# Row units of the attention scores: forty ahead of the attention steps instead of thirty-two, the other 216 spread evenly

## The chip, the cores and the metric

One NeuronCore of a Trainium2 chip runs the whole kernel. The metric is the device time of one execution in microseconds; the median of three runs of the kernel before is 518.95 us (518.05 to 519.51). Its engines work in parallel, each through its own queue in order: TensorE (PE in the profile) does matmuls into PSUM, VectorE (DVE) and ScalarE (ACT) read PSUM and compute elementwise, GpSimd (POOL) helps, and the DMA queues move data. They wait for each other on semaphores.

## The reference

One transformer layer on x, 1024 tokens by 512 features. With `xn = layernorm(x)` the result is `x + attention(xn) + ffn(xn)`:

```
q, k, v = bitnet_linear(xn, ...)     # sign(weight) matmul, times mean|weight| * scale
                                     # 32 query heads, 8 key/value heads, head size 16
attn    = softmax(q @ k.T / sqrt(16))
out     = bitnet_linear(attn @ v, o_weight, o_scale)
ffn     = (silu(xn @ gate.T) * (xn @ up.T)) @ down.T      # 1792 hidden features
```

The softmax of each query row subtracts that row's maximum over the 1024 keys, so the maxima have to be known before the exponentials are taken.

## The kernel before, in words

**Two stages.** The front does the layernorm, the projections of q, k and v, and the gate and up matmuls of the feed-forward part. The attention steps follow, then the output projection and the down projection.

**Row units.** Heads are taken in 8 groups of 4 query heads that share a key head; a group is two half-blocks of 512 queries, so there are 16 blocks. Before a block's scores can be shifted by their row maxima, the maxima are computed by 16 *row units*, 256 in all. A unit `A n` is 128 queries of one head against all 1024 keys: two matmuls of 512 keys (line 1081, `half_rows`, one in the upper and one in the lower half of the array's rows) into one of two pairs of PSUM banks (unit number modulo 2), then one VectorE reduction of 128x1024 (line 796, `row_max`). The semaphore `rows_ready` releases the reduction; `rows_free` releases the matmuls of unit n once the reduction of unit n-2 is done, since it uses the same bank pair. When all 16 maxima of a block are there, `transpose_max` (line 1092) turns them, ScalarE copies them (line 582), and two GpSimd operations split them.

**Attention steps.** There are 128 steps, 8 per block. A step (`scores`, `exps`) has four score matmuls (line 1165), each 128 keys by 512 queries into one of three banks, four exponentials on ScalarE (line 663), and the products of the probabilities of the step before with the values (`times_values`, line 1200; 16 records a step, in two halves). Score and row matmuls alternate between the halves of the array's rows. At the end of each block ScalarE copies the products out (line 674). In the 112 steps of the first seven groups the kernel also computes, two units a step, the row units of the next group: the first unit's matmuls stand beside scores 0 and 1, the second's beside scores 2 and 3. The last 16 steps have no row units; parts of the down projection fill them.

**The order of the front.** It is written out by hand, one string for TensorE (`pe_order`), one for VectorE (`dve_order`) and one for ScalarE. `F w` is a gate and an up half (16 matmuls of 512 columns, line 1072; on VectorE line 891, on ScalarE lines 644 and 576). `S 1` sums the magnitudes of the output weights with an fp32 matmul (line 1012) into bank 0 and makes the output scale on VectorE (lines 862, 864 and 867); `SUM_AT` is the first unit behind it, whose matmuls wait for `factors_ready`, which line 864 gives, because they write bank 0 again. `T 0` is the transposition of block 0's maxima, into bank 6. The feed-forward unit w waits for the VectorE result of unit w-2 (`h_ready`), and the one behind `T 0` also for ScalarE's copy of the maxima (`max_taken`). The first attention step's scores wait for `h_ready` too, its third one for all 28.

Of the kernel before, what the change touches and what calls it, by code (L numbers as in the profile page):

```python
# [27 lines left out]
def layer_kernel(nc, x, wq, wk, wv, wo, sq, sk, sv, so, gate, up, down, sg, su, sd, out,  # L28
# [18 lines left out]
    NG = NKV  # L47
    NP = NG // 2
    STEPS = 2 * TT
    FU = 2 * FT  # L50

    assert KV == P and HC * P == H and QT * P == NH * D and TT % 4 == 0
# [6 lines left out]
    pe_order = ("K0 X0 X1 X2 X3 K1 S0 X4 X5 G0 X6 Z0 X7 U0 P0 Z1 P1 Z2 G1 P2 U1 F2 F3 P3 F4 P4 F5 P5 F6 F7 A0 F8 F9 "  # L59
                "A1 A2 F10 F11 A3 A4 F12 A5 A6 F13 A7 S1 F14 A8 A9 F15 A10 A11 F16 A12 A13 F17 A14 A15 F18 A16 F19 "  # L60
                "A17 A18 F20 T0 A19 A20 F21 A21 A22 F22 A23 F23 A24 A25 F24 A26 A27 F25 A28 A29 F26 A30 A31 F27 ")
    dve_order = ("M0 M1 J0 M2 M3 H0 M4 R0 N0 J1 N1 M5 N2 N3 M6 M7 H1 L0 R1 L1 N4 N5 L2 L3 S0 Z0 N6 N7 J2 L4 V0 L5 L6 "
                 "Z1 L7 F0 Z2 g0 G0 Z3 X0 g1 F1 G1 E2 F2 X1 F3 g2 G2 g3 G3 F4 g4 F5 X3 G4 F6 F7 A0 g5 F8 G5 F9 X4 "
                 "F10 A1 A2 A3 F11 A4 X5 A5 A6 F12 A7 S1 F13 A8 F14 A9 F15 A10 A11 F16 A12 A13 A14 F17 A15 A16 F18 "
                 "F19 A17 A18 A19 A20 F20 F21 A21 F22 A22 A23 F23 A24 A25 F24 A26 A27 A28 A29 F25 F26 A30 A31 F27 ")
    act_order = ("D0 B0 C0 B1 B2 D1 C1 C2 N2 C3 C4 C5 W0 C6 N0 C7 F0 N1 E0 E1 X0 F1 F2 X1 Y0 F3 E3 F4 V2 E4 F5 X3 F6 "
# [16 lines left out]
    for order in (pe_order, dve_order):  # L83
        assert [n for kind, n in order if kind == "A"] == list(range(2 * UNITS))
    assert [n for kind, n in act_order if kind == "F"] == list(range(FU))
# [36 lines left out]
    def exps_before(e):  # L122

        return e - 2 if e - 3 < T_ENTRY else max(e - 3, T_ENTRY)

    def at(gp, s):
# [5 lines left out]
    with ExitStack() as ctx:  # L132
# [573 lines left out]
        def _(dve):  # L706
# [86 lines left out]

            def row_max(n, hf, idx):
                dve.wait_ge(rows_ready, n + 1)
                nc.vector.tensor_reduce(nmx[:, hf, idx:idx + 1], bank_pair(idx % 2), AX.X, ALU.max,  # L796
                                        negate=True).then_inc(rows_free, 1)

            splits = 0
            for kind, n in dve_order:  # L800
# [84 lines left out]
                elif kind == "F":  # L885
                    f, hf = n // 2, n % 2
                    dve.wait_ge(gt_ready, n + 1)
                    dve.wait_ge(up_ready, n + 1)
                    if n >= 2:
                        dve.wait_ge(hlo_ready, n - 1)  # L890
                    nc.vector.scalar_tensor_tensor(out=hb[:, n % 2, :], in0=ps[:, 5 + 2 * (n % 2), :],  # L891
                                                   scalar=usc[:, f:f + 1], in1=gt[:, n % 2, :],
                                                   op0=ALU.mult, op1=ALU.mult).then_inc(h_ready, 1)
                elif kind == "V":


                    dve.wait_ge(factors_ready, 2)
                    step(nc.vector.tensor_reduce(vg[:, 0:1], svb[:, :], AX.X, ALU.max, apply_absolute_value=True))
                    step(nc.vector.tensor_scalar(vg[:, 1:2], vg[:, 0:1], float(H), TOP, ALU.mult, ALU.min))
                    step(nc.vector.tensor_scalar(vg[:, 2:3], vg[:, 1:2], TINY, 1.0 / VTOP, ALU.max, ALU.mult))  # L900
                    nc.vector.reciprocal(vg[:, 3:4], vg[:, 2:3]).then_inc(vscale_ready, 1)
                elif kind == "A":
                    row_max(n, n // UNITS, n % UNITS)

            def step_rows(gp, s, last):

                gp_, par, hf, j = at(gp, s)
                with_rows = not (last and (par == 1 or s == 2 * STEPS))
                ga_ = gp_ * 2 + par + 1
                if with_rows:  # L910
                    row_max(ga_ * (2 * UNITS) + hf * UNITS + 2 * j, hf, 2 * j)
                    row_max(ga_ * (2 * UNITS) + hf * UNITS + 2 * j + 1, hf, 2 * j + 1)

# [35 lines left out]

            step_rows(0, 0, False)  # L950
            for gp in range(NP - 1):
                for s in range(1, 2 * STEPS + 1):
                    step_rows(gp, s, False)
            for s in range(1, 2 * STEPS):
                step_rows(NP - 1, s, True)
                if s in O_INVERT:
                    invert(O_INVERT.index(s))
                if s in O_NORM:
                    normalize_output(O_NORM.index(s))
                if s in O_SPLIT:  # L960
                    o_low(O_SPLIT.index(s))
                if s in D_OUT:
                    down_out(D_OUT.index(s))
# [12 lines left out]
        def _(pe):  # L976
# [99 lines left out]

            def half_rows(par, hf, idx, b):

                head, qt = idx // (HALF // P), idx % (HALF // P)
                low = b * HI  # L1080
# [3 lines left out]

            def rows(n, par, hf, idx):
                pe.wait_ge(rows_free, n + 1)
                half_rows(par, hf, idx, 0)
                half_rows(par, hf, idx, 1).then_inc(rows_ready, 1)

# [4 lines left out]
            for kind, n in pe_order:  # L1094
# [15 lines left out]
                elif kind == "A":  # L1110
                    if n == 0:
                        pe.wait_ge(y_ready, len(PROJ))
                        pe.wait_ge(kA_loaded[0], 32)
                    if n % UNITS == 0:
                        pe.wait_ge(q_loaded[0][n // UNITS], 32)
                    if n == SUM_AT:
                        pe.wait_ge(factors_ready, 3)
                    rows(n, 0, n // UNITS, n % UNITS)
                elif kind == "T":
# [18 lines left out]
            def scores(gp, s, last, opening=False):  # L1138
# [8 lines left out]
                with_rows = not (last and par == 1)  # L1147
                if with_rows and j == 0:
                    pe.wait_ge(q_loaded[1 - par][hf], 32 * (gp_ + par + 1))
                    if hf == 0:  # L1150
                        pe.wait_ge(kA_loaded[1 - par], 32 * (gp_ + par + 1))
                if not with_rows:
                    fill = list(range(len(FILLS) * (s - STEPS) // STEPS, len(FILLS) * (s - STEPS + 1) // STEPS))
                transposes = not (last and s >= STEPS + TT)
                for i, r in enumerate(ROUND):
# [7 lines left out]
                    if opening and i == 2:  # L1163
# [3 lines left out]
                                     qst[low:low + SROWS, par, hf, r, :], start=True, stop=True).then_inc(scores_ready, 1)  # L1167
                    idx = 2 * j + i // 2
                    if with_rows and i < REP - 1:
                        if i % 2 == 0:  # L1170
                            pe.wait_ge(rows_free, (gp_ * 2 + par + 1) * (2 * UNITS) + hf * UNITS + idx + 1)
                        mm = half_rows(1 - par, hf, idx, 1 - half)
                        if i % 2 == 1:
                            mm.then_inc(rows_ready, 1)
                        if i == REP - 2:
                            half_rows(1 - par, hf, idx, half).then_inc(rows_ready, 1)
                    if i % 2 == 1 and with_rows and not opening:
# [110 lines left out]
```

## Time and profile before

| | |
|---|---|
| median of 3 runs | 518.95 us |
| profiled execution | 519.96 us, of which 518.2 us lie between its first and last instruction (the span) |
| TensorE busy | 493.8 us (95%) |
| VectorE busy | 418.3 us (81%), of it 293.3 us in the 256 reductions |
| ScalarE busy | 351.1 us (68%), of it 274.2 us in the 512 exponentials |
| chain that ended last | 83% TensorE, 7% ScalarE, 4% VectorE |

The span is from the first to the last instruction; 1.76 us of the profiled execution lie around it. Records overlap: a matmul of 512 columns is shown with some 380 ns, while the next one starts 216 ns behind it, so distances between starts tell the pace, not the mean durations. The same holds for a reduction, shown with 1.21 us. In this execution the front reaches to 160.59 us, where the first score matmul starts; the last step with row units ends near 420 us.

### The profile page before, as it was taken

How to read it: one execution, taken by the hardware profiler on the slowest of the kernel's cores; microseconds unless marked ns; L12 is line 12 of the kernel's file. 1: busy time of each engine (PE TensorE's matmuls, PEld its weight loads, DVE VectorE, ACT ScalarE, POOL GpSimd, SP SyncE). 2: the span in 40 equal slices, each digit the busy share in tenths (PEclk: the TensorE clock that was granted, in tenths of full speed). 3: DMA queues.
4: the chain of work that ended last, by engine and by line, in shares of the span. 5: the costliest groups of instructions: out<-in, count | busy, mean ns of one | idle time of the engine just before them, and what ended most of it. 6: DMA issues, size and time to landing. Idle time of an engine off the chain costs nothing.

```text
span 518.2 us, 9807 instructions
## 1 busy us (share of the span) xinstructions
PE 493.8 (95%) x3928; PEld 170.9 (33%) x3928; DVE 418.3 (81%) x483; ACT 351.1 (68%) x639; POOL 97.4 (19%) x140
## 2 busy tenths in 40 slices
PE   2899999999999999999999999999999999999995
PEld 1866444433432222222222222222222222223442
DVE  7459866876678999999999999999999942224795
ACT  2373545222337999999999999999999986774000
POOL 4200424744424000000000000000000121241031
PEclk9999999999999999999999999999999999999999
DMA  8901482443100911202102120110210214451321
GB/s 278 214 2 59 119 198 44 102 79 43 22 1 7 165 34 42 60 23 61 40 25 59 40 60 23 53 47 24 61 40 23 66 44 114 95 170 48 98 82 40
DMA packets 29956, 36.37 MB, mean 70 GB/s; under 512 B 6544, under 2 KB 20752, under 8 KB 29912
## 3 DMA queue, kind: packets, MB, share of 16 engines
q1 hardware_dynamic: 20888, 24.72, 16.0%
q0 software_dynamic: 8304, 10.95, 11.1%
q8 instruction: 31, 0.51, 0.4%
q10 hardware_dynamic: 720, 0.08, 0.1%
q14 instruction: 13, 0.11, 0.1%
HBM read 30.62 MB, written 10.35 MB: 79 GB/s over the span
## 4 chain that ended last, share of the span: by engine, by line
PE 83%; ACT 7%; DVE 4%; DMA 3%; issue 2%; SPq 1%; ACTq 0%; DVEq 0%
PE ps L1200 23%; PE ps L1072 19%; PE ps L1165 14%; PE ps L1133 9%; PE ps L1081 8%; ACT room L663 5%; PE ps L1051 3%; PE ps L1226 3%; DVE nmx L796 3%; PE ps L1004 2%; DMA room<-wq 2%; ACT osb L674 1%; DMA ga<-r_scratch 1%; PE ps L1043 1%; SPq L384 1%
## 5 line engine op out<-in xcount | busy, mean ns | idle before, releaser
L796 DVE TENSOR_REDUCE nmx<-ps 128x1 f32<-128x1024 f32 x256 | 293.3, 1213 | 9.9 <-PE ps L1081 9.7
L663 ACT ACTIVATE room<-ps 128x512 f32<-128x512 f32 x512 | 274.2, 597 | 21.3 <-PE ps L1165 11.2
L1200 PE MATMUL ps<-room,vcur 128*32 128x256 f32 (+1 forms) x1912 | 160.0, 406 | 4.4 <-ACT osb L674 4.2
L1165 PE MATMUL ps<-qst,kB 50*128 50x512 f16 x512 | 150.2, 383 | 2.5 <-ACT room L663 1.8
L1081 PE MATMUL ps<-kA,qst 48*128 48x512 f16 x512 | 145.3, 382 | 0.0
L1072 PE MATMUL ps<-room,wf 128*128 128x512 f16 x448 | 101.5, 381 | 0.0
L1200 PEld LDWEIGHTS ps<-room,vcur 128*32 128x32 f32 x1912 | 37.7, 108 | 99.9 <-issue 52.7
L1165 PEld LDWEIGHTS ps<-qst,kB 50*128 50x128 f16 x512 | 30.9, 93 | 114.5 <-ACT room L663 101.5
L644 ACT ACTIVATE room<-ps,gsc 128x512 f32<-128x512 f32 x28 | 19.2, 686 | 63.6 <-PE ps L1072 63.6
L1072 PEld LDWEIGHTS ps<-room,wf 128*128 128x128 f16 x448 | 42.5, 98 | 55.4 <-issue 8.0
L502 POOL TENSOR_TENSOR hlo<-room,hhi 128x512 f16<-128x512 f32 x28 | 34.1, 1216 | 98.2 <-ACT hhi L576 98.2
L508 POOL TENSOR_TENSOR shp<-mxs,ones 16x128 f16<-16x128 f32 x16 | 7.2, 448 | 226.9 <-ACT mxs L582 226.9
L1133 PE MATMUL ps<-wd,hhi 128*128 128x512 f16 x112 | 42.6, 380 | 0.0
L1133 PE MATMUL ps<-wd,hlo 128*128 128x512 f16 x112 | 42.5, 380 | 0.0
L891 DVE SCALAR_TENSOR_TENSOR room<-ps,usc,room 128x512 f32<-128x512 f32 x28 | 20.9, 747 | 21.5 <-PE ps L1072 10.7
L924 DVE TENSOR_TENSOR y<-y,ga 128x1024 f32<-128x1024 f32 (+1 forms) x5 | 5.1, 1012 | 33.4 <-DMA ga<-r_scratch 33.4
L1081 PEld LDWEIGHTS ps<-kA,qst 48*128 48x128 f16 x512 | 27.2, 94 | 7.5 <-issue 6.7
L576 ACT CAST hhi<-room 128x512 f16<-128x512 f32 x28 | 17.1, 610 | 2.1 <-DVE room L891 2.1
L1051 PE MATMUL ps<-room,sgn 128*128 128x512 f16 x80 | 18.0, 379 | 0.0
L1133 PEld LDWEIGHTS ps<-wd,hhi 128*128 128x128 f16 x112 | 10.9, 98 | 13.2 <-issue 1.8
L1133 PEld LDWEIGHTS ps<-wd,hlo 128*128 128x128 f16 x112 | 10.9, 98 | 13.1 <-issue 1.8
L461 POOL TENSOR_TENSOR room<-room,parts 128x512 f32<-128x512 f32 x6 | 8.5, 1421 | 35.3 <-DVE room L936 29.6
(128 smaller groups left out, 289.2 us busy)
## 6 DMA issues: line engine op xcount, KB each, us to landing
qst<-q_scratch SPq DMA_DIRECT2D x32, 192.0 KB, 3.4
o_scratch<-osb SPq DMA_DIRECT2D x16, 256.0 KB, 2.3
q_scratch<-parts SPq DMA_DIRECT2D x12, 256.0 KB
hlo<-x SPq DMA_DIRECT2D x8, 256.0 KB, 4.7
parts<-x POOLq DMA_DIRECT2D x8, 256.0 KB, 2.9
wf<-gate POOLq DMA_DIRECT2D x14, 128.0 KB, 3.7
wf<-up POOLq DMA_DIRECT2D x14, 128.0 KB, 4.0
wd<-down POOLq DMA_DIRECT2D x1, 1792.0 KB, 13.7
```

What stands on the lines that cost most here:

```text
L502: nc.gpsimd.tensor_tensor(hlo[:, f, hf * HALF:(hf + 1) * HALF], hb[:, w % 2, :], hhi[:, f, hf * HALF:(hf + 1) * HALF], ALU.subtract).then_ ...
L576: nc.scalar.copy(hhi[:, f, hf * HALF:(hf + 1) * HALF], hb[:, n % 2, :]).then_inc(hhi_ready, 1)
L644: nc.scalar.activation(gt[:, n % 2, :], ps[:, 4 + 2 * (n % 2), :], ACT.Silu, scale=gsc[:, f:f + 1]).then_inc(gt_ready, 1)
L663: nc.scalar.activation(probs[:, s % 2, r, :], ps[:, score_bank(entry(j, i)), :], ACT.Exp, scale=gam_reg[par][r]).then_inc(scores_free, 1)
L796: nc.vector.tensor_reduce(nmx[:, hf, idx:idx + 1], bank_pair(idx % 2), AX.X, ALU.max, negate=True).then_inc(rows_free, 1)
L891: nc.vector.scalar_tensor_tensor(out=hb[:, n % 2, :], in0=ps[:, 5 + 2 * (n % 2), :], scalar=usc[:, f:f + 1], in1=gt[:, n % 2, :], op0=ALU. ...
L1051: mm = nc.tensor.matmul(ps[:, 2 * (n % 2) + hf, :], sgn[:, c, c0:c0 + P], xs[:, c, hf * HALF:(hf + 1) * HALF], start=(c == 0 and xs is xhi ...
L1072: mm = nc.tensor.matmul(ps[:, 4 + 2 * (w % 2) + z, :], wf[:, f % WF_BUFS, z, c * P:(c + 1) * P], xs[:, c, hf * HALF:(hf + 1) * HALF], star ...
L1081: return nc.tensor.matmul(ps[:, 2 * (idx % 2) + b, :], qst[low:low + KROWS, par, hf, head, qt * P:(qt + 1) * P], kA[low:low + KROWS, par, ...
L1133: mm = nc.tensor.matmul(ps[:, i, :], (hhi, hlo)[part][:, f, i * P:(i + 1) * P], wd[:, f, :], start=(f == 0 and part == 0), stop=(f == FT - ...
L1165: nc.tensor.matmul(ps[:, score_bank(e), :], kB[low:low + SROWS, par, kt % (TT // 2) * P:(kt % (TT // 2) + 1) * P], qst[low:low + SROWS, pa ...
L1200: mm = nc.tensor.matmul(ps[32 * r:32 * r + 32, 7, of], vcur[:, par, key_tile(r, j), :], probs[:, s % 2, r, of], start=(j == 0 and part == ...
```

## The change

The number of row units in the front goes from 32 to 40 (`AHEAD = 8`), so the front also computes half of block 2's. The remaining 216 units are dealt to the 112 steps by a formula: step t gets the units from 40 + 216 t / 112 up to 40 + 216 (t+1) / 112, rounded down. That is two units in 104 steps and one unit in eight: steps 0, 14, 28, 42, 56, 70, 84 and 98. Block, half and buffers of a unit now follow from its number (`row_block`), and the waits for the loaded queries and keys go with the unit that needs them first (`rows_loaded`). In the strings of the front, the units from A8 on are placed in pairs, two between every two F, and their neighbours change at three places, shown below. The core of the diff:

```diff
+    AHEAD = 8
...
-    pe_order: "... A5 A6 F13 A7 S1 F14 A8 A9 F15 ... A17 A18 F20 T0 A19 A20 F21 ... A30 A31 F27"
+    pe_order: "... A5 A6 F13 A7 S1 A8 A9 F14 A10 A11 F15 ... F20 A22 A23 T0 A24 A25 F21 ... A36 A37 F27 A38 A39"
...
+    ROW_STEPS = (NG - 1) * STEPS
+    OPEN_ROWS, ALL_ROWS = 2 * UNITS + AHEAD, NG * 2 * UNITS
+
+    def row_units(t):
+
+        first, end = [OPEN_ROWS + (ALL_ROWS - OPEN_ROWS) * (t + e) // ROW_STEPS for e in range(2)]
+        return list(range(first, end)) if t < ROW_STEPS else []
...
-            step_rows(0, 0, False)
+            step_rows(0, 0)
...
+            def rows_loaded(n):
+
+                gp, par, hf, idx = row_block(n)
+                if idx == 0:
+                    pe.wait_ge(q_loaded[par][hf], 32 * (gp + 1))
+                    if hf == 0:
+                        pe.wait_ge(kA_loaded[par], 32 * (gp + 1))
...
+                units = row_units(gp * (2 * STEPS) + s)
+                for n in units:
+                    rows_loaded(n)
...
-                    idx = 2 * j + i // 2
-                    if with_rows and i < REP - 1:
+                    if i < REP - 1 and i // 2 < len(units):
+                        n = units[i // 2]
                         if i % 2 == 0:
-                            pe.wait_ge(rows_free, (gp_ * 2 + par + 1) * (2 * UNITS) + hf * UNITS + idx + 1)
-                        mm = half_rows(1 - par, hf, idx, 1 - half)
-                        if i % 2 == 1:
+                            pe.wait_ge(rows_free, n + 1)
+                        mm = half_rows(n, 1 - half)
+                        if i == REP - 2:
+                            mm = half_rows(n, half)
+                        if i > 0:
                             mm.then_inc(rows_ready, 1)
-                        if i == REP - 2:
-                            half_rows(1 - par, hf, idx, half).then_inc(rows_ready, 1)
```

(The two lines of `pe_order` are cut to the places that change their neighbours. VectorE's string follows: behind `A7 S1` it now has A8 and A9 ahead of F13, at the transposition `F19 A22 A23 F20 A24 A25 F21`, and at the end `F26 A36 A37 F27 A38 A39`.)

TensorE at S 1, before. Line 1012 is S 1, lines 1072 are a feed-forward unit, lines 1081 the row units A7 (above) and A8, A9 (below).

```order
L1081 MATMUL ps<-kA,qst 128x512
L1012 MATMUL ps<-room,ones 128x512 [waits rows_free,mag_ready]
L1072 MATMUL ps<-room,wf 128x512 [waits h_ready,xlo_ready,wf_loaded3]
L1072 MATMUL ps<-room,wf 128x512 x15
L1081 MATMUL ps<-kA,qst 128x512 [waits rows_free,factors_ready]
L1081 MATMUL ps<-kA,qst 128x512
L1081 MATMUL ps<-kA,qst 128x512 [waits rows_free]
```

The same place in the changed kernel, where S 1 is line 1025, a feed-forward unit 1085 and a row unit 1095.

```order
L1095 MATMUL ps<-kA,qst 128x512
L1025 MATMUL ps<-room,ones 128x512 [waits rows_free,mag_ready]
L1095 MATMUL ps<-kA,qst 128x512 [waits rows_free,factors_ready]
L1095 MATMUL ps<-kA,qst 128x512
L1095 MATMUL ps<-kA,qst 128x512 [waits rows_free]
L1095 MATMUL ps<-kA,qst 128x512
L1085 MATMUL ps<-room,wf 128x512 [waits h_ready,xlo_ready,wf_loaded3]
```

The sixteen matmuls of F14 stood between S 1 and the wait for `factors_ready`; now they stand behind it.

TensorE at the transposition (line 1092), before: F20, T 0, then A19 and A20, then F21.

```order
L1072 MATMUL ps<-room,wf 128x512 x15
L1092 MATMUL ps<-ident,nmx 16x128 [waits rows_free,h_ready]
L1081 MATMUL ps<-kA,qst 128x512 [waits rows_free]
L1081 MATMUL ps<-kA,qst 128x512
L1081 MATMUL ps<-kA,qst 128x512 [waits rows_free]
L1081 MATMUL ps<-kA,qst 128x512
L1072 MATMUL ps<-room,wf 128x512 [waits h_ready,max_taken,xlo_ready,wf_loaded2]
```

The same place after (line 1114 is T 0): F20, A22, A23, T 0, A24, A25, F21.

```order
L1085 MATMUL ps<-room,wf 128x512 x15
L1095 MATMUL ps<-kA,qst 128x512 [waits rows_free]
L1095 MATMUL ps<-kA,qst 128x512
L1095 MATMUL ps<-kA,qst 128x512 [waits rows_free]
L1095 MATMUL ps<-kA,qst 128x512
L1114 MATMUL ps<-ident,nmx 16x128 [waits rows_free,h_ready]
L1095 MATMUL ps<-kA,qst 128x512 [waits rows_free]
L1095 MATMUL ps<-kA,qst 128x512
L1095 MATMUL ps<-kA,qst 128x512 [waits rows_free]
L1095 MATMUL ps<-kA,qst 128x512
L1085 MATMUL ps<-room,wf 128x512 [waits h_ready,max_taken,xlo_ready,wf_loaded2]
```

Two more units stand between F20 and F21, so four share two bank pairs with no feed-forward unit between them.

TensorE where the steps open, before: F27, then step 0 (line 1165 scores, each but the last with row matmuls behind it).

```order
L1072 MATMUL ps<-room,wf 128x512 x15
L1165 MATMUL ps<-qst,kB 128x512 [waits kB_loaded0,q_loaded10,shift_loaded00,kA_loaded1,q_loaded00,scores_free,kones_ready,h_ready]
L1081 MATMUL ps<-kA,qst 128x512 [waits rows_free]
L1165 MATMUL ps<-qst,kB 128x512 [waits scores_free]
L1081 MATMUL ps<-kA,qst 128x512
L1165 MATMUL ps<-qst,kB 128x512 [waits h_ready,scores_free]
L1081 MATMUL ps<-kA,qst 128x512 [waits rows_free]
L1081 MATMUL ps<-kA,qst 128x512
```

After: F27, A38 and A39, then step 0 (line 1184 scores) with the single unit A40.

```order
L1085 MATMUL ps<-room,wf 128x512 x15
L1095 MATMUL ps<-kA,qst 128x512 [waits rows_free]
L1095 MATMUL ps<-kA,qst 128x512
L1095 MATMUL ps<-kA,qst 128x512 [waits rows_free]
L1095 MATMUL ps<-kA,qst 128x512
L1184 MATMUL ps<-qst,kB 128x512 [waits shift_loaded00,kB_loaded0,q_loaded00,scores_free,kones_ready,h_ready]
L1095 MATMUL ps<-kA,qst 128x512 [waits rows_free]
L1184 MATMUL ps<-qst,kB 128x512 [waits scores_free]
L1095 MATMUL ps<-kA,qst 128x512
L1184 MATMUL ps<-qst,kB 128x512 [waits h_ready,scores_free]
L1184 MATMUL ps<-qst,kB 128x512 [waits scores_free] x2
```

In front of step 0's second score stands the wait of A40 for the reduction of A38, which was issued just ahead; scores 2 and 3 have no row matmuls beside them.

## Rows read from the trace of the kernel before

**Rows 1.** Busy time of each engine by stretch: front, opening, steps.

```profile
core 0: us, PE busy (x) PEld busy (x) DVE busy (x) ACT busy (x) POOL busy (x), PEclk, DMA share, GB/s
82.00:160.00 78.00, 78.00 (x375) 31.17 (x374) 58.34 (x63) 26.49 (x43) 34.92 (x37) 1.00 0.24 45
...
182.00:402.40 220.40, 216.53 (x2320) 54.90 (x2316) 218.52 (x193) 211.87 (x409) 12.41 (x30) 1.00 0.15 42
```

**Rows 2.** Order of time, TensorE, within a block: start, us, instruction, [idle before].

```profile
247.93 0.64 PE L1200 MATMUL ps<-room,vcur 128*32 128x256 f32 x8
248.50 0.39 PE L1165 MATMUL ps<-qst,kB 50*128 50x512 f16 x1
248.51 0.60 PE L1081 MATMUL ps<-kA,qst 48*128 48x512 f16 x2
248.74 0.38 PE L1165 MATMUL ps<-qst,kB 50*128 50x512 f16 x1
249.04 0.64 PE L1200 MATMUL ps<-room,vcur 128*32 128x256 f32 x8
```

**Rows 3.** Order of time, VectorE, one block of 16 reductions.

```profile
221.94 18.21 DVE L796 TENSOR_REDUCE nmx<-ps 128x1 f32<-128x1024 f32 x16 [0.16 <-PE ps L1081]
```

**Rows 4.** Order of time, ScalarE, in the same steps and at block ends.

```profile
247.82 1.09 ACT L663 ACTIVATE room<-ps 128x512 f32<-128x512 f32 x2
...
248.99 0.60 ACT L663 ACTIVATE room<-ps 128x512 f32<-128x512 f32 x1
...
255.44 0.59 ACT L674 COPY osb<-ps 128x512 f32<-128x512 f32 x1
...
273.82 0.59 ACT L674 COPY osb<-ps 128x512 f32<-128x512 f32 x1
```

**Rows 5.** Order of time, TensorE at S 1 and behind it.

```profile
103.14 1.13 PE L1012 MATMUL ps<-room,ones 128*128 128x512 f32 x2
104.10 3.62 PE L1072 MATMUL ps<-room,wf 128*128 128x512 f16 x16
107.65 0.61 PE L1081 MATMUL ps<-kA,qst 48*128 48x512 f16 x4
108.18 3.63 PE L1072 MATMUL ps<-room,wf 128*128 128x512 f16 x16
```

**Rows 6.** Order of time, VectorE at S 1.

```profile
104.39 0.68 DVE L862 TENSOR_SCALAR ga<-ps 128x512 f32<-128x512 f32 x1
105.10 0.75 DVE L864 SCALAR_TENSOR_TENSOR sob<-sob,vg,ga 128x512 f32<-128x512 f32 x1
```

**Rows 7.** Order of time, TensorE and VectorE at T 0, and a front pair's reductions.

```profile
131.92 0.27 PE L1092 MATMUL ps<-ident,nmx 128*16 128x128 f32 x1
132.12 0.61 PE L1081 MATMUL ps<-kA,qst 48*128 48x512 f16 x4
132.66 3.63 PE L1072 MATMUL ps<-room,wf 128*128 128x512 f16 x16
...
132.56 2.35 DVE L796 TENSOR_REDUCE nmx<-ps 128x1 f32<-128x1024 f32 x2 [1.47 <-PE ps L1081]
```

**Rows 8.** Order of time, TensorE, VectorE and ScalarE where the steps open.

```profile
160.59 0.39 PE L1165 MATMUL ps<-qst,kB 50*128 50x512 f16 x1
...
161.65 0.37 PE L1165 MATMUL ps<-qst,kB 50*128 50x512 f16 x1 [0.45 <-DVE room L891]
...
163.98 0.64 PE L1200 MATMUL ps<-room,vcur 128*32 128x256 f32 x8 [0.19 <-ACT room L663]
...
160.75 0.75 DVE L891 SCALAR_TENSOR_TENSOR room<-ps,usc,room 128x512 f32<-128x512 f32 x1 [1.08 <-issue]
...
161.80 2.04 ACT L663 ACTIVATE room<-ps 128x512 f32<-128x512 f32 x4
```

**Rows 9.** Waits of TensorE and busy time by stretch near the start.

```profile
PE ps L983 <- DVE room L744: 4.0, 1, 4.0
...
0.00:40.00 40.00, 28.53 (x135) 21.97 (x136) 24.32 (x70) 17.14 (x22) 8.96 (x21) 1.00 0.57 160
```

## What the change will do: the prediction

> **What bounds the kernel now.** I read four views: busy time by stretch, to see which engines are full; the order of time within a block, for the true pace of each; the order of time at the three places where neighbours change; and the waits. By stretch [rows 1], TensorE is full in the front (78.00 of 78.00 us), while VectorE is not (58.34). Whatever is put on TensorE's queue there, work or waiting, comes out at the end one for one. In the steps three engines look full: TensorE 216.5, VectorE 218.5 and ScalarE 211.9 of 220.4 us. Busy shares can't say which of them sets the pace, so the distances between starts must.
>
> A half step on TensorE goes from products to products, 247.93 to 249.04: 1.11 us, with no idle time shown [rows 2]. In it two scores and two row matmuls take 0.54 us (248.50 to 249.04), which is two matmuls one behind the other and not four: each score shares its time with a row matmul in the other half of the array's rows (starts 0.01 apart). The sixteen reductions of a block take 18.21 us [rows 3], so they follow each other at (18.21 - 1.21) / 15 = 1.133 us. They are slower than TensorE's 1.11 and fall behind inside a block by 16 x 0.023 = 0.4 us; the two bank pairs take this up, and at the block's end TensorE waits for ScalarE's copy and VectorE catches up (0.16 us idle [rows 3]). A block lasts 273.82 - 255.44 = 18.38 us [rows 4]: 16 x 1.11 = 17.76 and 0.6 for copy and transposition. If reductions set the pace, the half steps would be 1.13 apart, and they are 1.11. So I take TensorE as the bound, VectorE just behind it (18.13 + 0.16 of 18.38) and ScalarE also near.
>
> **The change part by part.** Three terms lengthen the front, one lengthens the opening of the steps, one shortens the steps.
>
> *First, work in the front.* Behind S 1 and ahead of F27 stand 30 units instead of 24. A pair of units takes 108.18 - 107.65 = 0.53 us on TensorE [rows 5]. Three more pairs are 1.6; they stand at one place more between feed-forward units, 0.1 for the change between the two kinds of matmul (an estimate; below 0.2 in any case, since a whole pair costs 0.53). Together 1.7 us. VectorE hides their reductions: a pair takes 2.35 [rows 7] and its feed-forward product 0.7, in a period of 3.55 + 0.53 = 4.08 us.
>
> *Second, the wait at S 1.* A8 waits for `factors_ready`, since it writes the bank that S 1 filled. Line 864 gives it at 105.10 + 0.75 = 105.85 [rows 6]. F14 started at 104.10, right behind S 1, and covered this completely [rows 5]. Now A8 stands there, and everything behind it in TensorE's queue with it: 105.9 - 104.1 = 1.8 us lost. Nothing else could run, for the queue is in order.
>
> *Third, the wait at T 0.* Without F between them, A22 to A25 share two bank pairs. Counted from A22's first matmul, the reductions begin after 132.56 - 132.12 = 0.44 and take 2.35 for two [rows 7]: done at 1.65 and 2.79. A25 needs the second, so it starts at 2.8 and F21 some 0.3 behind it, at 3.1. Unhindered the two pairs and T 0 would take 0.54 + 0.20 + 0.54 = 1.28 [rows 7]. Loss 1.8 us. `max_taken` is long there by then.
>
> So F27 ends 1.7 + 1.8 + 1.8 = 5.3 us later than in the profile before.
>
> *Fourth, the opening.* Before, the first score starts right at F27's end (160.59), and ScalarE takes exponentials from 161.80 on without a break, four in 2.04 us [rows 8]. Counting from F27's end, the product of F27 is at 0.16 on VectorE [rows 8]; behind it the reduction of A38 starts at 0.8 and ends at 2.05. A40 waits for it, and score 1 stands behind A40: it starts at 2.1 and is ready at 2.5, where ScalarE could have taken it at 1.2 + 0.5 = 1.7. The next ones follow 0.5 apart, so the exponentials of step 0 come 0.8 us late, and step 1's products with them. Step 0 has one unit only, so VectorE, which has A38 to A42 to do from 0.8 on, is through with A41 at 0.8 + 4 x 1.13 = 5.3, before step 2 asks for it (near 6): no further loss. I take 0.8 (0.3 if ScalarE catches up with its spacing of 0.48 against 0.55 in the steps, 1.5 if A41 and A42 hold TensorE too).
>
> *Fifth, the eight steps with one unit.* Step 0 is counted. In the other seven, scores 2 and 3 stand alone, in different halves, and can run side by side: at most 0.22 us of TensorE's 0.54 goes. But the products wait for the last exponential of the step before: two exponentials end at 247.82 + 1.09 = 248.91 [rows 4], and the products begin at 249.04 [rows 2]. Of 0.13 some 0.1 is to be had. 7 x 0.09 = 0.6 us; bounds 0 (it is lost at the next copy) and 7 x 0.22 = 1.5. The eight reductions that leave, 8 x 1.13 = 9 us of VectorE, buy nothing more, since it isn't the bound.
>
> The waits for queries and keys that now come up to four steps (9 us) earlier cost nothing: queries are reloaded when their block's scores are done, and the new units need them half a block (9.2 us) later.
>
> The sum is 5.3 + 0.8 - 0.6 = 5.5 us. Against the profiled execution, 519.96, of which 1.76 lie around the span, it gives 525.5; the median of the runs is 1.0 us below that execution, so I predict 518.95 + 5.5 = 524.4 us. With the ends of each term (front 4.3 to 6, opening 0.3 to 1.5, steps -1.5 to 0) the case reaches from 522.3 to 526.3.
>
> **The rivals.**
>
> *Reductions set the steps' pace (faster).* For it: VectorE is busy 99% of the steps [rows 1], with 0.16 us idle a block [rows 3]. If TensorE's half step is only as short as the bank pairs allow, the 216 units take 8 x 1.13 = 9.0 us less than the 224, and 524.4 + 0.6 - 9.0 = 516.0 comes out. It decides from the point where more than 6 of the 9 us are given back, at any of the seven steps. Against it: the half steps lie 1.11 apart, which is less than a reduction. Chance 0.06. The Trainium skill, "TensorEngine Tiling (Array Packing)", section Performance Considerations, says the same as this rival in general: tiling makes TensorE faster but not the emptying of PSUM, so the read of PSUM may become the bottleneck. By that rule 516 would come; rows 2 and 3 put TensorE first by 0.02 us a half step.
>
> *One of the two waits doesn't arise.* If the units around T 0 or at S 1 find what they need in time, 1.8 us go: 522.6, and without both 520.8. For S 1 line 864 would have to be faster than shown; for T 0 the reductions. Neither has a reason in the rows. Chance 0.08.
>
> *TensorE's clock falls in the waits.* If it were granted the lower of its levels, 1.2 instead of 2.4 GHz, behind each wait, the sixteen matmuls that follow (3.55 us [rows 5]) would take 3.5 us longer each: 524.4 + 7 = 531. Against it: a wait of 4.0 us near the start left the granted clock at 1.00 [rows 9]. Chance 0.03. [...]
>
> The forecast itself has 0.83.
>
> **How the numbers follow.** A run of this kernel can be told from no change at about 0.3%, 1.6 us: 517.4 to 520.5. Faster: the rival with the reductions, 0.06. Same: part of the case without both waits and of a half-true reduction rival, 0.03. Slower: the rest, 0.91. The range goes from 521.3, so that it takes in the case with one wait missing, to 526.3; what is left out is the reductions, part of the second rival and the clock, and some 0.05 of larger terms than I see.
>
> **What would show it.** In the profile after: TensorE waits of 1.8 us for VectorE line 881 behind line 1025, and of 0.9 and 0.8 us for reductions (line 813) in front of A24 and A25, between F20 and F21; the first score (line 1184) near 166.5; the second one 1.5 us behind it; blocks of 18.37 us without a one-unit step and 0.1 less with one; VectorE idle about 1.1 us at each such step. I am wrong if blocks become shorter than 18.2 throughout (reductions were the bound), or if the front ends before 164 (the waits are not there).

## The result, and the profile after

The changed kernel is slower: 528.73 us median of six runs (527.21 to 531.89) against 519.88 us of the kernel before in the same comparison. The ratio is 1.0164, with its 95% interval [1.0136, 1.0193], so 8.5 us, where 5.5 was forecast, and the time lies above the range (521.3 to 526.3). The profiled execution took 531.89 us, of it 530.1 span. It is the longest of the six.

The busy line and the clock line of the page of after (40 slices of 13.25 us; a 9 stands for 90% or more):

```profile
PE 500.8 (94%) x3928; PEld 172.4 (33%) x3928; DVE 420.0 (79%) x483; ACT 351.8 (66%) x639; POOL 97.5 (18%) x140
...
PEclk9999999999899799999999999999999998999999
```

Three slices are below 9, where the kernel before had none: at about 138, 173 and 442 us. The busy time by stretch, of the first two and of what lies between them, and then of the steps (columns as in [rows 1], the granted clock third from the end):

```profile
138.50:141.80 3.30, 3.30 (x9) 1.18 (x8) 1.71 (x2) 1.19 (x2) 0.00 (x0) 0.50 0.06 9
141.90:172.50 30.60, 28.56 (x147) 10.73 (x145) 22.88 (x23) 11.40 (x20) 9.33 (x11) 1.00 0.01 1
172.60:179.30 6.70, 6.70 (x41) 1.25 (x41) 4.14 (x4) 4.12 (x9) 3.25 (x5) 0.50 0.53 77
...
193.00:413.00 220.00, 215.64 (x2302) 55.28 (x2302) 212.30 (x186) 211.66 (x409) 12.43 (x30) 1.00 0.15 41
```

A granted clock of 0.50 is the lower level, 1.2 GHz. In the steps the clock is full again and VectorE has fallen from 99% to 96.5% busy.

Who waited, TensorE in after (us in total, times, longest):

```profile
PE ps L1219 <- ACT osb L690: 4.4, 13, 0.5
...
PE ps L1095 <- DVE nmx L813: 2.9, 3, 1.3
PE ps L1184 <- ACT room L679: 2.1, 2, 1.6
PE ps L1095 <- DVE sob L881: 1.7, 1, 1.7
```

The kernel before has no waits for the reductions (there line 796) or for the S 1 product (line 864). They are the waits of the forecast, at its three places. In order of time, TensorE at S 1 and at T 0 (compare [rows 5, 7]):

```profile
103.05 1.12 PE L1025 MATMUL ps<-room,ones 128*128 128x512 f32 x2
105.83 0.60 PE L1095 MATMUL ps<-kA,qst 48*128 48x512 f16 x4 [1.65 <-DVE sob L881]
106.37 3.63 PE L1085 MATMUL ps<-room,wf 128*128 128x512 f16 x16
...
134.51 0.60 PE L1095 MATMUL ps<-kA,qst 48*128 48x512 f16 x4
135.04 0.28 PE L1114 MATMUL ps<-ident,nmx 128*16 128x128 f32 x1
136.22 0.39 PE L1095 MATMUL ps<-kA,qst 48*128 48x512 f16 x2 [0.90 <-DVE nmx L813]
137.35 0.39 PE L1095 MATMUL ps<-kA,qst 48*128 48x512 f16 x2 [0.74 <-DVE nmx L813]
137.67 5.31 PE L1085 MATMUL ps<-room,wf 128*128 128x512 f16 x16
142.92 0.61 PE L1095 MATMUL ps<-kA,qst 48*128 48x512 f16 x4
```

A8 starts 2.78 us behind S 1 instead of 0.96. F21 starts 3.16 us behind A22, where 3.1 was worked out. But then F21 takes 142.92 - 137.67 = 5.25 us where every other one takes 3.56: half the clock for 3.4 us costs 1.7.

Where the steps open (compare [rows 8]), and the first steps:

```profile
167.94 0.38 PE L1184 MATMUL ps<-qst,kB 50*128 50x512 f16 x1
169.60 0.39 PE L1095 MATMUL ps<-kA,qst 48*128 48x512 f16 x2 [1.28 <-DVE nmx L813]
169.83 0.59 PE L1184 MATMUL ps<-qst,kB 50*128 50x512 f16 x3
...
173.50 1.08 PE L1219 MATMUL ps<-room,vcur 128*32 128x256 f32 x8
...
179.60 0.64 PE L1219 MATMUL ps<-room,vcur 128*32 128x256 f32 x8
```

Score 1 comes 1.9 us behind score 0, where 1.5 was forecast. At 173.50 the products take 1.08 us and at 179.60 again 0.64: half the clock in between.

The steps themselves. A half step with two scores and no row unit, and the next ones:

```profile
236.85 0.64 PE L1219 MATMUL ps<-room,vcur 128*32 128x256 f32 x8
237.42 0.42 PE L1184 MATMUL ps<-qst,kB 50*128 50x512 f16 x2
237.77 0.64 PE L1219 MATMUL ps<-room,vcur 128*32 128x256 f32 x8
238.34 0.39 PE L1184 MATMUL ps<-qst,kB 50*128 50x512 f16 x1
...
238.98 0.64 PE L1219 MATMUL ps<-room,vcur 128*32 128x256 f32 x8
...
240.09 0.64 PE L1219 MATMUL ps<-room,vcur 128*32 128x256 f32 x8
```

The first half step is 0.92 us instead of 1.11, the next one 1.21 and then 1.11 again: 0.19 won, 0.10 given back at the next step's products. VectorE in a block without a one-unit step and behind one, and ScalarE's copies at the ends of another block (compare [rows 3, 4]):

```profile
214.18 18.22 DVE L813 TENSOR_REDUCE nmx<-ps 128x1 f32<-128x1024 f32 x16 [0.15 <-PE ps L1095]
...
239.02 11.66 DVE L813 TENSOR_REDUCE nmx<-ps 128x1 f32<-128x1024 f32 x10 [0.72 <-PE ps L1095]
```

```profile
265.97 0.59 ACT L690 COPY osb<-ps 128x512 f32<-128x512 f32 x1
...
284.26 0.59 ACT L690 COPY osb<-ps 128x512 f32<-128x512 f32 x1
```

284.26 - 265.97 = 18.29 us is a block with a one-unit step (42) in it, 0.09 less than the 18.38 of before; blocks without one stay at 18.37. VectorE idles 0.72 us at a one-unit step (1.1 was forecast), and the block is not shorter by that.

Comparing every step's first exponential in the two traces, counted from S 1's first matmul, gives where the time of the three profiles is, 9.1 to 12.0 us at their ends:

| place (us) | profile of after | second and third profile | forecast |
|---|---|---|---|
| F27's last matmul | +7.0 | +7.0, +7.0 | +5.3 |
| of it, F21 at half clock | 1.7 | 1.7, 1.7 | |
| opening, step 0 to 1 | +1.1 | +1.1, +1.1 | +0.8 |
| opening, steps 1 to 3 | +2.7 | +1.2, +1.2 | 0 |
| one-unit steps | -0.54 | -0.55, -0.51 | -0.6 |
| steps 112 to 118 | +2.0 | +0.5, -0.1 | 0 |

### The profile page after: what moved, and what is told of

Read it like the earlier page. It is cut to its first block, busy times and chain, and to the rows that moved or that the text cites. A ratio compares the mean times of both kernels' runs of the same rounds, so it can differ in the third digit from the quotient of the medians.

```text
span 530.1 us, 9807 instructions
## 1 busy us (share of the span) xinstructions
PE 500.8 (94%) x3928; PEld 172.4 (33%) x3928; DVE 420.0 (79%) x483; ACT 351.8 (66%) x639; POOL 97.5 (18%) x140
## 4 chain that ended last, share of the span: by engine, by line
PE 77%; ACT 10%; issue 5%; DMA 3%; DVE 2%; POOL 1%; SPq 1%; ACTq 0%; POOLq 0%; DVEq 0%
PE ps L1219 21%; PE ps L1085 19%; PE ps L1184 12%; ACT room L679 9%; PE ps L1095 8%; PE ps L1153 7%; PE ps L1064 3%; PE ps L1245 3%; PE ps L1017 2%; DMA room<-wq 2%; DMA ga<-r_scratch 1%; ACT osb L690 1%; DVE nmx L813 1%; PE ps L1056 1%; SPq L400 1%
## 5 line engine op out<-in xcount | busy, mean ns | idle before, releaser
L1085 PE MATMUL ps<-room,wf 128*128 128x512 f16 x448 | 103.0, 385 | 0.0
L937 DVE TENSOR_TENSOR y<-y,ga 128x1024 f32<-128x1024 f32 (+1 forms) x5 | 5.1, 1012 | 32.3 <-DMA ga<-r_scratch 32.3
L477 POOL TENSOR_TENSOR room<-room,parts 128x512 f32<-128x512 f32 x6 | 8.6, 1427 | 35.2 <-DVE room L949 29.7
```

Of the source, the lines that this page charges most:

```text
L1085: mm = nc.tensor.matmul(ps[:, 4 + 2 * (w % 2) + z, :], wf[:, f % WF_BUFS, z, c * P:(c + 1) * P], xs[:, c, hf * HALF:(hf + 1) * HALF], star ...
```

## Experiments

**The change again, twice.** The same kernel.

> The changed kernel once more, for one more profile. Theory 1 (a wait makes the lower clock likely just behind it): stretches at half clock again behind T 0 or in the opening, each costing about half its length, and none in the dense part of the front. Theory 2 (chance): half-clock stretches anywhere. Without them 525.5 us.

> The changed kernel again, on one chip with the three below. Theory 1: before plus 8 to 9 us, of it 5.5 to 6.5 at full clock; half-clock stretches behind T 0 and in the opening.

Measured: 528.37 us in one run; and 528.46 us median (528.23 to 529.84), ratio 1.0146 [1.0127, 1.0166]. Both profiles have the half-clock stretches in the same two places; those of the third profile:

```profile
138.20:141.40 3.20, 3.20 (x9) 1.20 (x8) 1.81 (x2) 0.84 (x2) 0.00 (x0) 0.50 0.14 22
172.30:175.50 3.20, 3.20 (x21) 0.65 (x17) 1.79 (x2) 2.19 (x6) 2.48 (x3) 0.50 0.11 7
```

Here the one in the opening is half as long, and the span 527.0. The third stretch, near 442, is missing in both. The first two places come back in each of three profiles, so chance in place is as good as excluded for them, not for the third.

**TensorE kept busy in the three waits.**

```diff
                     if n == SUM_AT:
+                        pe.wait_ge(wf_loaded[3], 64)
+                        pe.wait_ge(h_ready, 13)
+                        fill_wait(14, 0, 8)       # 8 matmuls of 512 columns, result unused
                         pe.wait_ge(factors_ready, 3)
+                    if n in (24, 25):
+                        pe.wait_ge(wf_loaded[2], 96)
+                        pe.wait_ge(h_ready, 20)
+                        fill_wait(21, 1, 4)
...
+                        if opening and i == 0:
+                            pe.wait_ge(h_ready, FU)
+                            # 5 matmuls of kA with qst into bank 7, result unused
```

> The changed kernel with the same three waits, but TensorE runs matmuls nobody reads while it waits: eight behind S 1, four each ahead of A24 and A25, five ahead of A40 in step 0. Theory 1 (the idle time makes the chip grant the lower clock, and the waits themselves cost what was predicted): granted clock near 0.999, time the kernel before plus 5.5 us, some 524.5. Theory 2 (the clock falls by chance, whatever TensorE does): like the changed kernel, before plus 8.5 to 10 us, clock 0.98 to 0.99. Theory 3 (the waits cost more than was predicted, whatever the clock): before plus 8 with the clock at 1.00.

Measured: profile of 524.1 us span (525.81 us) with granted clock 0.999; 526.73 us median of six (524.1 to 528.54), ratio 1.0122 [1.0091, 1.0152]. TensorE around T 0 (line 1119 is the filling):

```profile
133.88 0.60 PE L1095 MATMUL ps<-kA,qst 48*128 48x512 f16 x4
...
134.53 1.03 PE L1119 MATMUL ps<-room,wf 128*128 128x512 f16 x4
135.59 0.39 PE L1095 MATMUL ps<-kA,qst 48*128 48x512 f16 x2
135.91 1.04 PE L1119 MATMUL ps<-room,wf 128*128 128x512 f16 x4
136.88 0.39 PE L1095 MATMUL ps<-kA,qst 48*128 48x512 f16 x2
137.21 3.63 PE L1085 MATMUL ps<-room,wf 128*128 128x512 f16 x16
140.77 0.61 PE L1095 MATMUL ps<-kA,qst 48*128 48x512 f16 x4
```

and the same two stretches as in the profile above:

```profile
138.20:141.40 3.20, 3.20 (x18) 1.19 (x16) 1.86 (x3) 1.19 (x2) 0.98 (x1) 1.00 0.00 0
172.30:175.50 3.20, 3.20 (x36) 0.82 (x36) 2.85 (x3) 2.99 (x6) 1.39 (x4) 1.00 0.60 86
```

F21 starts 3.33 us behind A22 (3.16 without the filling), so the waits last at least as long. F21 takes 3.56 us again, and the clock is full in both places. So in the profiles the lost clock hangs on the idle time, not on the new order. F27 ends 5.5 us later than before (forecast 5.3), step 1 is 1.07 us later still, and the steps give back 0.5: 6.0 us at full clock, near the sum of the forecast (5.5). The median of the six, 6.3 us above the kernel before by the ratio, is not the 524.5 that was expected.

The medians need care. Beside the changed kernel on one chip, with 5 runs each:

> The changed kernel with TensorE kept busy in all three waits, again, to have it beside the changed kernel on one chip. Theory 1: 2 to 3 us below the changed kernel. Theory 2 (the clock falls by chance, whatever TensorE does in the waits): the same time as the changed kernel.

Measured: 528.52 us (526.81 to 530.15), ratio 1.0156 [1.0135, 1.0177], the same as the changed kernel's 1.0146. This expectation failed. Two more profiles were to tell where such executions lose their time.

> The changed kernel with TensorE kept busy in its three waits, one more profile. If idle time is what lets the clock fall: no half-clock stretch behind S 1 or T 0 and none in the opening; what it loses lies near 437 us, behind a wait of 1 to 1.7 us that every kernel of this study has, or near the start. If the clock falls by chance: a stretch behind T 0 or in the opening.

> The same kernel and the same question as the run before it: a stretch behind T 0 or in the opening would speak for chance, one near 437 us or none for the idle time.

Measured: 527.52 and 526.85 us. In all four profiles of this kernel there is no stretch at S 1, at T 0 or in the opening. Two of them (fill_b, fill_c) have one at 437 us, behind a wait for ScalarE in step 115, which is not from the change. In fill_c:

```profile
434.41 0.39 PE L1197 MATMUL ps<-qst,kB 50*128 50x512 f16 x1
436.49 0.39 PE L1197 MATMUL ps<-qst,kB 50*128 50x512 f16 x1 [1.69 <-ACT room L679]
...
438.07 0.63 PE L1166 MATMUL ps<-wd,hhi 128*128 128x512 f16 x1
438.50 0.63 PE L1166 MATMUL ps<-wd,hlo 128*128 128x512 f16 x1
```

That costs 1.6 us. From S 1 to step 111 the four filled profiles are 6.0 us behind the kernel before, the three of the changed kernel 8.7 to 10.3. The times do not show this gain. Over all runs, 13 of the filled kernel average 527.5 us, 12 of the changed one 528.8, and 60 of the kernel before 520.8, but these averages mix chips; on the one chip where both ran, five runs of each average 528.7 us. The granted clocks of the five filled ones are 0.981 to 0.995, those of the changed kernel 0.980 to 0.992, so the filled ones lost clock too. Only one of the five was profiled, so where the others lost it stays open.

**Only the waits at T 0 filled.** As above, without the filling at S 1 and in the opening.

> The changed kernel with matmuls nobody reads only in the two waits beside T 0 (four ahead of A24, four ahead of A25); the waits at S 1 and in the opening stay idle. Theory 1: F21 takes 3.55 us instead of 5.25, so 1.5 to 1.7 us below the changed kernel, with half-clock stretches in the opening still. Theory 2: the same time as the changed kernel, F21 at 5.25 in the profile.

Measured: 528.74 us median (526.77 to 533.6), ratio 1.0165 [1.0133, 1.0196], so the expected gain of 1.5 to 1.7 us does not show in the time. The profile has what was expected of it: F27 ends 5.5 us later instead of 7.0, no stretch behind T 0, and one of 6.8 us in the opening, where this kernel idles as the changed one does.

```profile
130.00:160.00 30.00, 29.96 (x147) 11.67 (x145) 22.70 (x23) 8.73 (x15) 8.93 (x11) 1.00 0.07 10
167.50:174.20 6.70, 6.33 (x37) 1.19 (x37) 4.59 (x5) 5.21 (x11) 3.44 (x5) 0.50 0.29 30
```

**Fewer units ahead.** `AHEAD` 6, 4 and 2; the pairs move up, so that each smaller one drops a wait.

```diff
-    AHEAD = 8    # S1 A8 A9 F14 ... F20 A22 A23 T0 A24 A25 F21 ... F27 A38 A39
+    AHEAD = 6    # S1 A8 A9 F14 ... F20 T0 A22 A23 F21     ... F27 A36 A37
+    AHEAD = 4    # S1 F14 A8 A9 ... F20 T0 A20 A21 F21     ... F27 A34 A35
+    AHEAD = 2    # S1 F14 A8 A9 ... F20 T0 A20 A21 F21     ... F26 A32 A33 F27
```

> 38 units in front: the wait at S 1 stays, A36 and A37 stand behind F27, but T 0 has only one pair beside it. Theory 1: the wait at T 0 (1.8 us) and one pair (0.54) go, so before plus 3.3 us, plus what the clock still costs at the opening (0 to 3 us). Theory 3: before plus 6 or more.

Measured: 524.93 us, ratio 1.0093 [1.0069, 1.0116], 4.8 us. Front 2.8, step 1 another 1.07, steps -0.35, clock full in the front and the opening in its profile. That profiled run is the shortest of the six, 521.93 us; what the others lost was not profiled.

> 36 units in front: F14 again covers S 1, T 0 has one pair, A34 and A35 stand behind F27. Only the opening is as in the changed kernel. Theory 1: before plus 1.1 us by the work and the wait, and if the idle time at the opening is enough for the lower clock, 3 more; the granted clock tells which. Theory 2: before plus 4 or so at any place.

> 36 units in front, only the opening as in the changed kernel, one more profile: a half-clock stretch in the opening again if its idle time of 1.3 us is enough, front plus 0.4 us and step 1 plus 1.5 at full clock.

Measured: 521.87 us median of 12, with one disturbed run of 2549 us (521.46 without it); ratio 1.0039 [1.0010, 1.0067], 2.0 us; the single run took 522.09. The front is 0.43 longer, step 1 is 1.07 later, and a half-clock stretch in the opening adds 1.2 in both profiles. The second one's:

```profile
164.00:167.30 3.30, 3.30 (x25) 0.62 (x17) 2.02 (x2) 2.39 (x6) 2.29 (x3) 0.50 0.08 1
```

> 34 units in front and no new wait at all: F14 covers S 1, one pair at T 0, nothing behind F27. Theory 1: before plus 0.3 to 0.5 us (one more pair of row units, 0.5, less a step with one unit), clock 0.999. Theory 2: a clock below 0.99 here too, and before plus 3 or more.

Measured: 521.13 us, ratio 1.0012 [0.9992, 1.0033], no difference that can be told; in its profile the front is 0.43 longer and nothing moves in the steps, as expected (0.3 to 0.5).

**One wait at a time in the kernel before.**

```diff
-  S1 F14 A8 A9 F15                 # TensorE, before
+  S1 A8 A9 F14 F15                 # before_s1
-  F25 A28 A29 F26 A30 A31 F27
+  F25 A28 A29 F26 F27 A30 A31      # before_open
```

> The kernel before, with A8 and A9 moved ahead of F14, straight behind S 1, and nothing else: the same work with one new wait. Theory 1: before plus 1.7 us, 3.4 if the clock falls behind it in most executions. If the wait were covered by something else: no difference.

Measured: 522.91 us, ratio 1.0038 [1.0001, 1.0074], 2.0 us.

```profile
101.87 1.12 PE L1012 MATMUL ps<-room,ones 128*128 128x512 f32 x2
104.64 0.61 PE L1081 MATMUL ps<-kA,qst 48*128 48x512 f16 x4 [1.65 <-DVE sob L864]
```

The wait is 1.65 us as in the changed kernel; F27 ends 1.72 later. No half clock follows S 1, but this profile has one in the opening, though nothing was changed there.

> The kernel before, with A30 and A31 moved behind F27: the same work, with the opening of the changed kernel but two units in step 0. By the waits alone: score 1 stands 1.5 us behind score 0 and step 2 waits for the reductions, before plus 0.5 to 1.5 us. With the lower clock in the opening, as in the changed kernel, up to 3 us more, and the profile shows the stretch near 165 us.

Measured: 525.31 us (519.99 to 526.2), ratio 1.0050 [1.0011, 1.0088]: 2.6 us by the ratio, 4.6 between the medians, since the runs fall apart into two groups. In its profile TensorE runs at half clock from 161.7 to 172.0 us, right behind the opening's waits, and step 3 comes 4.4 us later than before, though F27 ends 0.64 earlier. Four of the ten runs took 520.0 to 522.6 us and six 525.2 to 526.2, with the same instructions. The profiled run is one of the six; that the clock alone makes these 4 us is likely but not shown, since none of the four was profiled.

**The kernel before, for its own clock.**

> The kernel before once more, for one more profile. Earlier executions of it show granted clocks from 0.982 to 0.999 at nearly one time. Theory 1: where the clock is below 0.999, the half-clock stretch lies where TensorE is idle anyway (near the start) or in the opening and near 430 us, where waits of 0.4 and 1.2 us stand; time 518 to 522 us.

> The kernel before, one more profile: with 519 to 520.5 us no half-clock stretch between 30 and 500 us; with 521.5 or more one, in the opening or near 434 us.

Measured: 519.35 and 520.59 us. Both have a half clock near the start on record, the second another one at 430 us. The first one's:

```profile
16.80:26.80 10.00, 10.00 (x48) 10.00 (x48) 3.56 (x10) 1.28 (x3) 0.95 (x2) 0.50 0.86 211
```

The expectation for before_c (no stretch at such a time) did not hold: it has one at 430.3 to 433.7 us and gains the 1.6 us back by an early start, S 1 at 101.8 instead of 103.1. The stretch near the start costs it nothing against the kernel before: that one runs as slowly there, as is shown below.

**The kernel before, its own 0.45 us wait filled.** Three matmuls whose result nobody uses ahead of step 0's third score.

```diff
                     if opening and i == 2:
+                        pe.wait_ge(gt_ready, FU)
+                        # 3 matmuls of kA with qst into bank 6, result unused
                         pe.wait_ge(h_ready, FU)
```

> The kernel before with three matmuls nobody reads in the 0.45 us wait of step 0 ahead of its third score. If that short wait is what lets the clock fall in a third of its executions (those with 0.993 to 0.995): 0.3 to 0.7 us below the kernel before; if not, no difference, and 0.994 among its clocks as before. The added matmuls may themselves hold the third score by 0.2 us.

Measured: 520.26 us against 521.0, ratio 0.9983 [0.9966, 1.0000]. One of its 12 runs has a clock between 0.993 and 0.996, against 9 of the 17 of the kernel before beside it. That is as expected, but the gain of 0.9 us reaches to nothing within its interval, so it is not shown. It is the only version here with a ratio below 1.

**Where the profiles have the half clock.** All 18 profiles of the study; near the start and behind the last step not counted.

| place | TensorE idles there | half clock behind it |
|---|---|---|
| S 1, 1.65 us | after, after_b, after_c, fill_t0, ahead6, before_s1 | 0 of 6 |
| T 0, 0.90 and 0.74 us | after, after_b, after_c | 3 of 3 |
| T 0, filled | fill (4 profiles), fill_t0 | 0 of 5 |
| opening, 1.28 us and less | after (3), fill_t0, ahead4 (2), ahead6, before_open | 7 of 8 (not ahead6) |
| opening as before, 0.45 and less | before (3), ahead2, before_s1 | 1 of 5 |
| opening, filled | fill (4), before_fill | 0 of 5 |
| step 115, 1.56 to 1.83 us | 9 of the 18 | 8 of 9 |
| step 115, 1.11 to 1.55 us | the other 9 | 0 of 9 |

## Why the prediction was wrong

**What held.** The bound: TensorE sets the pace of the steps, the reductions do not; blocks stay at 18.37 us where no step has one unit, a one-unit step takes 0.09 us off a block and not a reduction's 1.13, and VectorE idles there. That refutes the rival with 516 us. The wait at S 1: 1.8 foreseen, 1.8 measured. The wait at T 0: F21 at 3.1 foreseen, 3.16 measured. The work of six more units: F27 ends 5.31 us late once F21's extra 1.69 are taken off, 5.3 foreseen. The seven one-unit steps: -0.54 against -0.6, six times 0.09 and nothing at step 56, which stands at a block's beginning and presumably loses its gain to the copy. The opening was mis-sized a little: 1.07 instead of 0.8. At full clock that is 5.8 us, and the profile of the filled kernel has 6.0, of it some 0.2 by the filling itself at T 0. The bounds of the forecast's sum are slightly off: the ends of its terms add up to 522.1 and 526.4 us, not 522.3 and 526.3; nothing hangs on it.

**The step that failed** is the rival "TensorE's clock falls in the waits", dismissed with a chance of 0.03. It was no rival but part of the likeliest case: in the three profiles the clock falls behind T 0 (1.7 us) and in the opening (1.2, 1.2 and 2.7 us), some 3 us on top of the waits. The reason given was [rows 9], a wait of 4.0 us near the start with the clock at 1.00, and that row was misread. The trace's record of the clock begins at 29.5 us, and the view counts as full what has no record. Before that the pace of the matmuls tells the clock, in the kernel before:

```profile
10.45 3.86 PE L983 MATMUL ps<-ident,room 128*128 128x128 f32 x16 [3.99 <-DVE room L744]
28.32 2.47 PE L1072 MATMUL ps<-room,wf 128*128 128x512 f16 x8
30.63 0.60 PE L983 MATMUL ps<-ident,room 128*128 128x128 f32 x4
32.35 1.89 PE L1072 MATMUL ps<-room,wf 128*128 128x512 f16 x8
```

Behind the wait of 4.0 us most matmuls of line 983 start 0.213 us apart, those at 30.63 us 0.109 apart. The first two of line 1072 start 0.43 us apart, those at 32.35 us 0.216. So TensorE ran at half its pace right behind that wait and up to some 29.5 us. The row was no evidence for a clock that holds through a wait (nor against it, for no row shows a higher clock ahead of that wait). All 18 profiles have this slow start, until 26.9 to 29.7 us. In nine, like before_b, the record begins at 13 to 15 us and shows 0.50 there (16.6 to 26.9 us in before_b); in nine, like before, it begins at 28.4 us or later. So the mean granted clock of an execution (0.982 to 0.999 for the kernel before) says in part only where the record begins: before_b has 0.988 and before 0.999, and from S 1 to step 114 they keep the same pace within 0.02 us.

The Trainium skill, "TensorE: Matmul & The Clock Gate", section Why this matters for your kernels, warns of idle gaps between bursts of matmuls that are longer than any of the waits at S 1, at T 0 and in the opening. The traces agree with it at S 1; at T 0 and in the opening the clock fell behind shorter waits than the page warns of, and there the measurement decides.

The size was wrong too: 3.5 us for each of two stretches. Behind T 0 it is 1.7, since a stretch lasts 3.4 us and half of it is lost. In the opening it is 1.2 (3.4 us) or 2.7 (6.8 us), less than half, perhaps because ScalarE is the one waited for in part of it, which no run tests. The two together, 2.9 in two of three profiles, on 5.8 at full clock make the 8.7 that these two profiles show at step 111. The median is 8.5 above the kernel before; that agreement is in part luck, since what the executions lose behind step 111 varies from -0.1 to 2.0 us up to step 118 alone.

**What stays open.** Why 1.65 us at S 1 never brought the clock down, while 0.90 and 0.74 us close together at T 0 did so each time, is not settled. At step 115 the longer waits are the ones with a stretch behind them (8 of the 9 from 1.56 us up, none of the 9 shorter), but 1.65 us at S 1 never had one, so the length of one wait does not decide it. Nor is it shown in time that the filling pays. That the stretches vanish with it is shown at T 0 (0 of 5 profiles, against 3 of 3) and in the opening of the changed kernel (0 of 4, against 7 of 8 where its wait stands unfilled); in before_fill the profile tells little, since the unfilled wait there had a stretch in 1 of 5. The stretch at 442 us in the profile of after is not from the change: the kernel before has it too.

The better orders tried here do not mend the change: a pair of units costs the front 0.43 to 0.64 us at full clock, and the two one-unit steps that it buys bring 0.18. The version with no new wait (34 units) is no faster than the kernel before.

## What to carry to other kernels

A unit of work that rides beside another matmul in the other half of the array is nearly free there (0.09 us here); moved to a stretch where TensorE has no slack it costs its full time (some 0.27 us here), however much it relieves an engine that is busy but not the bound. In a hand-written order, look at what stood between a producer and its consumer: the filler that is moved away was the cover of the wait. And count a wait on a full TensorE twice, once for itself and once for the clock behind it, unless several executions show that the clock holds. Read the clock from the pace of the matmuls too, for a view that shows it full may have no record of it there.

## What the runs showed of the hardware that was not expected

The granted clock fell to 0.50 behind waits of 0.45 to 1.8 us in otherwise full stretches, for 3.4, 6.8 or 10.2 us, and the same program has it in one execution and not in the next. F21's sixteen matmuls took 5.25 us instead of 3.56. Two scores in different halves of the array's rows with nothing beside them take 0.35 us up to the next products instead of 0.54, but only 0.09 of it is kept. A mean granted clock says little of the time by itself: before_b with 0.988 took 519.35 us and before with 0.999 took 519.96, since both start at half pace and only one has it on record, while 3.4 us in a full stretch cost 1.7.
